# A graph layer's destination rows: made per pair in the loop from copied columns of x, in place of a table and its loads

## What is computed

```python
def _cgconv(x, src, dst, edge_attr, Wf, bf, Ws, bs, gamma, beta, rmean, rvar):
    z = jnp.concatenate([x[dst], x[src], edge_attr], axis=-1)
    msg = jax.nn.sigmoid(z @ Wf + bf) * jax.nn.softplus(z @ Ws + bs)
    n = x.shape[0]
    summed = jax.ops.segment_sum(msg, dst, num_segments=n)
    cnt = jax.ops.segment_sum(jnp.ones((dst.shape[0],), x.dtype), dst, num_segments=n)
    out = summed / jnp.maximum(cnt, 1.0)[:, None]
    out = (out - rmean) * jax.lax.rsqrt(rvar + BN_EPS) * gamma + beta
    return out + x
...
x = _layernorm(x + _L0_gnn_ref(x, edge_index, edge_attr_64, ...), axis=-1)
```

## Time and profile before

| | |
|---|---|
| timed runs (3) | median 2142.03 us, 2137.26 to 2143.15 |
| span of the profiled execution | 2795.4 us |
| its own time beside the span | not given apart from the span |
| granted TensorE clock, mean | 0.747 |
| TensorE (PE) busy | 1618.1 us, 58% |
| VectorE (DVE) busy | 1685.4 us, 60% |
| ScalarE (ACT) busy | 1379.6 us, 49% |
| GpSimd (POOL) busy | 1541.2 us, 55% |
| moved by DMA | 401.73 MB, mean 144 GB/s |

### The profile page before, as it was taken

How to read it: one execution, slowest core, us unless ns; L and a number is a source line. 1 busy time by engine, 2 the same in 40 slices (tenths; PEclk the granted TensorE clock), 3 DMA queues, 4 the chain that set the end, 5 groups by cost and what they waited for, 6 DMA issues and landing times. The chain is left out here.

```text
span 2795.4 us, 33286 instructions
## 1 busy us (share of the span) xinstructions
PE 1618.1 (58%) x7507; PEld 1390.7 (50%) x7507; DVE 1685.4 (60%) x3576; ACT 1379.6 (49%) x2083; POOL 1541.2 (55%) x1590
## 2 busy tenths in 40 slices
PE   6565665566666666666726555555555454454554
PEld 5454555556555565555625444454444444454443
...
GB/s 314 124 148 136 135 147 143 138 151 137 138 143 145 151 145 144 138 155 129 224 152 138 133 138 138 135 144 127 144 138 131 134 138 137 131 144 135 133 136 62
DMA packets 232010, 401.73 MB, mean 144 GB/s; under 512 B 71586, under 2 KB 154906, under 8 KB 231863
## 3 DMA queue, kind: packets, MB, share of 16 engines
...
...
## 5 line engine op out<-in xcount | busy, mean ns | idle before, releaser
L333 POOL DMA_INDIRECT pre<-s_rows,ends x1568 | 1520.5, 970 | 1125.4 <-DVE soft_ps L584 557.2
L378 PE MATMUL pre_ps<-rhs,lhs 128*128 128x256 f32 x3136 | 1102.5, 513 | 1108.1 <-DVE lhs L564 581.1
L378 PEld LDWEIGHTS pre_ps<-rhs,lhs 128*128 128x128 f32 x3136 | 766.6, 256 | 1275.7 <-issue 685.3
L438 ACT ACTIVATE pre<-pre 128x512 f32<-128x512 f32 x392 | 247.5, 631 | 1323.7 <-DVE pre L580 1064.5
L600 DVE TENSOR_TENSOR sums<-sums,sum_ps 128x128 f32 (+1 forms) x784 | 196.4, 251 | 907.8 <-remote 765.2
L388 PEld LDWEIGHTS sum_ps<-hot,msg 128*128 128x128 f32 x3136 | 526.5, 230 | 49.9 <-DVE msg L591 7.3
L388 PE MATMUL sum_ps<-hot,msg 128*128 128x64 f32 x3136 | 489.2, 304 | 7.0 <-DVE msg L591 6.8
L580 DVE TENSOR_TENSOR pre<-pre_ps,pre 128x1024 f32<-128x1024 f32 x392 | 477.6, 1218 | 23.9 <-PE pre_ps L378 22.6
L443 ACT ACTIVATE logs<-pre 128x1024 f32<-128x1024 f32 x392 | 414.7, 1058 | 12.3
L564 DVE TENSOR_SCALAR lhs<-lhs,base_f,part 64x256 f32<-64x256 int32 x784 | 322.2, 454 | 48.1 <-issue 35.6
L591 DVE TENSOR_TENSOR msg<-soft_ps,logs 128x512 f32<-128x512 f32 x392 | 271.1, 692 | 13.3
...
## 6 DMA issues: line engine op xcount, KB each, us to landing
lhs<-dge_and_destination_cols SPq DMA_DIRECT2D x196, 512.0 KB
rhs<-d_rows SPq DMA_DIRECT2D x784, 64.0 KB
pre<-s_rows,ends POOLq DMA_INDIRECT x1568
s_rows<-pre SPq DMA_DIRECT2D x24, 512.0 KB, 5.6
d_rows<-logs SPq DMA_DIRECT2D x12, 512.0 KB
d_rows<-msg SPq DMA_DIRECT2D x8, 512.0 KB
...
d_rows<-hot SPq DMA_DIRECT2D x4, 512.0 KB
```

The source lines that it names most:

```text
L333: nc.gpsimd.indirect_dma_start(pre[:, slot(k, j), i, 0:F2], None, s_dram, bass.IndirectOffsetOnAxis(ap=ends[:, k, j * TILES + i, 0:1], axis=0)
L378: ins = nc.tensor.matmul(pre_ps[:, j % 2, i, :], lhs[:, j // 2, edges], rhs[:, j, i // 2, :], start=True, stop=True)
L438: nc.scalar.activation(pre[:, at, :, F2:3 * F], pre[:, at, :, F:F2], ACT.Abs).then_inc(s_abs[j], 1)
```

## The change

- `d_rows`, its 25 double tiles a layer, their bias adds, their stores and SP's loads of 64 rows a pair go.
- VectorE copies, four steps ahead, the 64 columns of x of each pair's window into `x_cols` (`window_cols`, at an address from a register), between and behind its two adds into `sums`. The registers of the next group's bases are read at the start of a group, beside those of the group before. The adds of both pairs now come ahead of L580.
- TensorE makes, two steps ahead (`dst_rows`), one product of the 128 copied columns (both pairs) with the destination weights, and one bf16 product that adds the bias out of three bf16 parts (`bias_b`), into `dst_ps`.
- ScalarE copies the two halves of `dst_ps`, 64x256 each, into `rhs` (`rows`). A copy keeps its partitions, so the first pair has its one-hot and destination rows on partitions 0 to 63 and the second on 64 to 127; the edge features and weights take the other half, and `edge_cols` is laid out so.
- `sum_ps` has one half only, and a window's sum waits for the adds of one step back in place of two. The counts of layer 1 are two matmuls of 2x64 columns in place of four of 64.
- SP stores all of `s_rows` before it reads the plan; the first edges are loaded behind the fourth store. GpSimd reads the plan before it waits for the stores.

The diff, cut to its core:

```diff
+LEAD = 2
...
+        x_cols = sb("x_cols", [P, SLOTS, PAIRS, WIN], F32)
         hot = sb("hot", [P, SLOTS, TILES, WIN], F32)
         msg = sb("msg", [P, SLOTS, TILES, F], F32)
         pre_ps = ps("pre_ps", [P, 2, TILES, F2], F32)
-        sum_ps = ps("sum_ps", [P, 2, PAIRS, 2, P], F32)
+        sum_ps = ps("sum_ps", [P, PAIRS, 2, P], F32)
         soft_ps = ps("soft_ps", [P, 2, TILES, F], F32)
+        dst_ps = ps("dst_ps", [P, F2], F32)
...
+        hot_rows = [slice(0, WIN), slice(FE, P)]
+        fea_rows = [slice(WIN, P), slice(0, FE)]
...
+        def ahead(g, j):
+            over = (j + LEAD) // SLOTS
+            return (g + over if over else g), (j + LEAD) % SLOTS
...
-            def load_rows(j, bases):
-                for q in range(PAIRS):
-                    sp.dma_start(rhs[FE:P, j, q, :], d_dram[bass.ds(bases[PAIRS * j + q], WIN), :]
-                                 ).then_inc(d_in[j], 16)
-
-
             for k in range(EARLY):
                 load_ends(k, k)
-            for c in range(8):
-                sp.wait_ge(s_copied, 2 * c + 2)
+            for c in range(STORES):
+                sp.wait_ge(s_copied, min(2 * c + 2, DOUBLES))
                 store_rows(sp, s_dram, s_stage, c, s_out)
+                if c == 3:
+                    for j in range(0, SLOTS, 2):
+                        load_edges(j, j * STEP)
             if first:
                 sp.wait_ge(table_out, 48)
             bodies = n_bodies(sp)
             at = sp.value_load(t["choice"][:, 1:2], min_val=0, max_val=GENERAL_AT * ROW)
-            load_table(at)
             for k in range(EARLY):
                 load_base(at + k * ROW, k)
-            for c in range(8, STORES):
-                sp.wait_ge(s_copied, min(2 * c + 2, DOUBLES))
-                store_rows(sp, s_dram, s_stage, c, s_out)
-            for j in range(0, SLOTS, 2):
-                load_edges(j, j * STEP)
-            for c in range(STORES):
-                sp.wait_ge(d_added, min(2 * c + 2, DOUBLES))
-                store_rows(sp, d_dram, d_stage, c, d_out)
-            for r in range(len(d_stage)):
-                sp.wait_ge(d_out[r], 16 * len(range(r, STORES, len(d_stage))))
+            load_table(at)
...
-                bases = entries(1, GPAIRS, NPAD - WIN)
...
-                    load_rows(j, bases)
-                    load_rows(j + 1, bases)
...
+            bodies = n_bodies(pool)
             for r in range(len(s_stage)):
                 pool.wait_ge(s_out[r], 16 * len(range(r, STORES, len(s_stage))))
-            bodies = n_bodies(pool)
...
+            def dst_rows(g, j):
+                done(pe, s_cols, g, j, 0)
+                done(pe, s_rows, g, j, 1)
+                nc.tensor.matmul(dst_ps[:], x_cols[:, j].rearrange("p q w -> p (q w)"), t["w_node"][:, layer - 1, 0:F2],
+                                 start=True, stop=False)
+                nc.tensor.matmul(dst_ps[:], t["ones_b"][:], t["bias_b"][:, layer - 1, :], start=False, stop=True
+                                 ).then_inc(s_dst[j], 1)
 
             def product(b, k, j):
                 g = group_no(b, k)
                 done(pe, s_hot_t, g, j, 0)
                 done(pe, edge_in, g, j // 2, 0, 16)
-                done(pe, d_in, g, j, 0, 16 * PAIRS)
+                done(pe, s_rows, g, j, 0)
...
-                done(pe, s_added, g, j, 2)
+                done(pe, s_added, g, j, 1)
                 for q in range(PAIRS):
                     for i in range(2):
-                        ins = nc.tensor.matmul(sum_ps[:, j % 2, q, 0, 0:WIN], msg[:, j, 2 * q + i, :],
+                        ins = nc.tensor.matmul(sum_ps[:, q, 0, 0:WIN], msg[:, j, 2 * q + i, :],
                                                hot[:, j, 2 * q + i, :], start=i == 0, stop=i == 1)
-                    if first:
-                        for i in range(2):
-
-                            ins = nc.tensor.matmul(sum_ps[:, j % 2, q, 1, 0:WIN], t["ones_b"][:],
-                                                   hot[:, j, 2 * q + i, :].bitcast(BF16)[:, 1::2],
-                                                   start=i == 0, stop=i == 1)
+                if first:
+                    halves = hot[:, j].bitcast(BF16).rearrange("p (q i) (w c) -> p q i w c", i=2, c=2)
+                    for i in range(2):
+                        ins = nc.tensor.matmul(sum_ps[:, :, 1, 0:WIN], t["ones_b"][:],
+                                               halves[:, :, i, :, 1], start=i == 0, stop=i == 1)
                 ins.then_inc(s_sum[j], 1)
...
+                    dst_rows(*ahead(group_no(b, k), j))
+            for j in range(LEAD):
+                dst_rows(0, j)
...
+            def rows(g, j):
+                done(act, s_dst, g, j, 0)
+                done(act, s_prod, g, j, SLOTS)
+                for q in range(PAIRS):
+                    ins = nc.scalar.copy(rhs[hot_rows[q], j, q, :], dst_ps[hot_rows[q], :])
+                ins.then_inc(s_rows[j], 1)
...
+                    rows(*ahead(g, j))
                     absolute(g, j, slot(k, j))
                     exponents(g, j, slot(k, j))
                     logarithms(g, j)
                     gate(g, j)
+            for j in range(LEAD):
+                rows(0, j)
...
+                then(nc.vector.memset(t["bias_b"][:], 0.0))
+                then(nc.vector.tensor_copy(parts[0], t["bias"][:]))
+                then(nc.vector.tensor_tensor(rest, t["bias"][:], parts[0], ALU.subtract))
+                then(nc.vector.tensor_copy(parts[1], rest))
+                then(nc.vector.tensor_tensor(rest, rest, parts[1], ALU.subtract))
+                then(nc.vector.tensor_copy(parts[2], rest))
+                for i, part in enumerate(parts):
+                    then(nc.vector.tensor_copy(t["bias_b"][32 * i:32 * i + 1], part[32 * i:32 * i + 1]))
+                v.sem_inc(bias_split, 1)
...
-                v.wait_ge(tables_done, DOUBLES + i + 1)
-                if c >= len(d_stage) and i % 2 == 0:
-                    v.wait_ge(d_out[c % len(d_stage)], 16 * (c // len(d_stage)))
-                nc.vector.tensor_tensor(d_stage[c % len(d_stage)][:, i % 2 * 2:i % 2 * 2 + 2, :],
-                                        table_ps[:, (DOUBLES + i) % 4],
-                                        t["bias"][:, layer - 1, :].unsqueeze(1).to_broadcast([P, 2, F2]), ALU.add
-                                        ).then_inc(d_added, 1)
...
-                    ins = nc.vector.tensor_scalar(lhs[WIN:P, j // 2, at], lhs[WIN:P, j // 2, at].bitcast(I32),
-                                                  base_f[WIN:P, k, PAIRS * j + q:PAIRS * j + q + 1],
-                                                  t["part"][WIN:P, 0:1], ALU.subtract, ALU.is_equal)
+                    ins = nc.vector.tensor_scalar(lhs[hot_rows[q], j // 2, at],
+                                                  lhs[hot_rows[q], j // 2, at].bitcast(I32),
+                                                  base_f[hot_rows[q], k, PAIRS * j + q:PAIRS * j + q + 1],
+                                                  t["part"][hot_rows[q], q:q + 1], ALU.subtract, ALU.is_equal)
...
-                ins = nc.vector.tensor_tensor(into, into, sum_ps[:, j % 2, q, 0:rows, 0:WIN], ALU.add)
+                ins = nc.vector.tensor_tensor(into, into, sum_ps[:, q, 0:rows, 0:WIN], ALU.add)
...
+            def window_cols(g, j, q, at):
+                if q == 0:
+                    done(v, s_dst, g, j, 0)
+                ins = nc.vector.tensor_copy(x_cols[:, j, q, :], x[:, bass.ds(at[PAIRS * j + q], WIN)])
+                if q == PAIRS - 1:
+                    ins.then_inc(s_cols[j], 1)
...
+                if live(0):
+                    window_cols(g, j, 0, cols_at)
+                if four_back:
+                    add_up(four_back[0], four_back[2], 1, sum_at)
+                if live(0):
+                    window_cols(g, j, 1, cols_at)
...
-                if four_back:
-                    add_up(four_back[0], four_back[2], 1, sum_at)
...
+            def base_loaded(k, turn):
+                if isinstance(turn, int):
+                    v.wait_ge(base_in[k], turn * 16 + 16)
+                else:
+                    v.wait_ge(base_in[k], turn * 16)
+                v.sem_inc(passed, 1)
...
+                if k < BODY - 1:
+                    base_loaded(k + 1, b if isinstance(b, int) else b + 1)
+                else:
+                    base_loaded(0, 1 if isinstance(b, int) else b + 2)
+                cols_at = load_bases((k + 1) % BODY)
...
+            base_loaded(0, 0)
+            cols_at = load_bases(0)
+            for j in range(SLOTS):
+                for q in range(PAIRS):
+                    ins = nc.vector.tensor_copy(x_cols[:, j, q, :], x[:, bass.ds(cols_at[PAIRS * j + q], WIN)])
+                ins.then_inc(s_cols[j], 1)
...
+    edge_cols = np.empty((P, EPAD // STEP, PAIRS, PAIR), features.dtype)
```

(2 more changed lines are left out.)

103 lines of the change are left out of this document (55 added, 48 removed).

## The result

The changed kernel takes 2136.47 us (median of 9 runs, 2131.03 to 2138.22), the kernel before beside it 2142.60 us (9 runs, 2137.26 to 2145.20): ratio 0.997, interval 0.9961 to 0.9979. That is 6.1 us or 0.3% faster. The forecast was 2122 us: its direction was right, the gain was less than a third of what it gave. Ratios and intervals leave out executions more than 1.5% above the fastest of their kernel, six of the twelve of `e1` among them; medians are of all.

A forecast was written before the change was run, and what follows sets the result against it. The prediction held that GpSimd's gathers, issued one after another at 5.01 us a step, bound the kernel. 2142 us less 10 for ring waits and 10 for earlier starts, all else 0, gave 2122 us, range 2085 to 2180.

The forecast's parts named there:

- the 765.2 us: VectorE's idle time ahead of the add into `sums` in the earlier profile; most of it held absent from timed runs.
- The gap of 25.1 us: What the median has above GpSimd's unstalled chain of 2116.9 us; to be filled by slow gathers and ring waits.
- slow gathers: Gathers taking 0.970 us in the mean instead of 0.95: 15 us taken of 31 possible.
- the ring: GpSimd's waits early in each layer, its seven slots full while the destination table is still being stored: 10 us taken.
- Term 1: Row loads, `d_rows` and its stores go; traffic was hidden, GpSimd's ring waits end: -10 us, between 0 and -39.
- Term 2: Start of each layer: source table stored sooner, first gather earlier: -5 us a layer, -10 together, between -14 and +3.
- Term 3: VectorE's two copies a step, added distance and register loads: 0, hidden by GpSimd's 5.01 us step; 196 us uncovered.
- Terms 4 to 6: TensorE's new products and ScalarE's copies, sums in one bank, bias parts and lane tables at the start: 0 each.
- this rival: TensorE at its lower clock for half the steps or more: 2138 us at half, 2436 at three quarters; chance 0.05.
- the 57 priced: Upper end for gathers slowed by starting under VectorE's copies: +57 us, 0 taken; as a rival 2179 us, chance 0.10.
- The rival "no difference": Timed ring waits were nil and the edge loads eat the earlier stores' gain: 2136 to 2148 us, chance 0.15.

The follow-up runs named there:

- e1: The kernel before with only the change's new order of stores and loads at the start, where the unaltered one takes 2789 us: 2781.74 us, ratio 0.9913.
- e16: The kernel before, unaltered, run again and traced on a chip like that of the comparison: 2140.09 us, ratio 0.9998.
- e18: The changed kernel with the old order at the start and the edge loads last: 2139.08 us, 0.9996 of the kernel before.
- e20: The changed kernel with VectorE making every second later copy of the source table's rows in place of ScalarE: 2133.92 us, 0.9977 of the kernel before.
- e10: The changed kernel with the first edge loads behind the last source store, where the kernel before takes 2789 us: 2841.30 us, ratio 1.0173.
- e15: The changed kernel with the bias product made twice in each step on TensorE: 2131.72 us, 0.9965 of the kernel before.

## Why the prediction was right in its direction and wrong in its size

- **What bounds the kernel: right.** GpSimd's chain of gathers does, on the chips of the comparison: 1568 gathers at 946 ns in the median with 0.30 us of issue, and only 10.2 us of other waits in the kernel before. The forecast had left out the 765.2 us as not being in a timed run. That is right for the timed runs shown, but not as it was meant, as something of the profiled execution: on the 2790 chips every traced execution has 653 to 765 us of them.
- **The gap of 25.1 us: filled with too much.** I put 15 us on slow gathers and 10 on the ring. In the trace of `e16` the layers take 990.47 + 989.69 us from first gather to last, 18.0 above 1566 x 1.253: 9.4 are slow gathers (1499.0 - 1568 x 0.95), 6.0 the ring's waits less their issue, and the rest is issue just over 0.30 us. Another 2.8 us lie behind the last gathers of the layers. (The waits taken whole would have passed the median by 45 us, not 46.) The 15.97 and 23.06 us of the earlier trace rows are 2.02 and 4.57 here.
- **Term 1, ring waits -10 us: the step that failed most.** The waits ended as said (10.2 to 0.3 us), but both layers together got only 2.6 us shorter, and in `e18` 0.3. A gather that had waited now has 0.30 us of issue like all others: 14 x 0.30 = 4.2 us were in those 10.2 anyway (issue, without the two starts, went from 472.6 to 476.8 us). And the gathers got slower, 1499.0 to 1502.4 us, 3.4 more. I had taken a wait whole and the disturbance at 0.
- **Term 2, an earlier start, -5 us in each layer: the mechanism right, the size too large in layer 2.** It gave 4.7 us in layer 1 and 2.5 in layer 2, less 1.1 us at the layers' ends, whose cause isn't shown. The pause at the choice did cost what it should, through the backlog of stores and not through a later last issue; that one is set by TensorE's 0.86 us for two tiles (`e20`). The other 1.4 and 1.2 us are the register that GpSimd reads ahead of its wait. The first gather came at 37.6 us, not 36: the last copy of the table ended at 30.8 instead of 29.5 us, and the store took 5.5 us behind the edge loads. `e10`, with the last copy at 29.8 us and no edge loads ahead, has it at 35.7. For layer 2 the forecast had no row, only layer 1's 5 us again.
- **Term 3, copies hidden: right, and its price was too high.** 222 ns each, within 70 to 280; uncovered 94.5 us for the copies and 123 in all, not 196. One wait of GpSimd for `soft_ps`, of 0.3 us, was left.
- **Terms 4 to 6 at 0: right** on a 2140 chip (for TensorE's part, `e15`). TensorE's two new products take 0.9 us a step ((263.7 + 109.0) / 396) and not 0.5, and are hidden all the same. The clock didn't fall: 0.832 before, 0.903 after, with TensorE's busy share at 73% instead of 70%. That is what the prediction had against this rival: TensorE has fewer idle stretches.
- **The gathers beside the copies.** They take 956 ns before and 958 after, and with each copy made twice 972 against 969 on a 2790 chip. 3.4 us of the 57 priced came, and hardly from the copies: in the trace of the changed kernel 102 gathers start under a copy, 948 ns in the mean, 970 at most. 2.5 of the 3.4 us lie on the gathers that start under `hot_transposed` (259 of 981 ns; before, 252 of 972). The Trainium skill, "SBUF — State Buffer", section "SBUF: two separate sides", would have fp32 copies lock GpSimd out; gathers that overlap a copy take 946.5 ns and those that don't 946.1 (without those that start under the one-hot rows), so the measurement decides against a sizeable price here.
- **The rival "no difference"** had the right range, and half of its reasons: the ring's waits were nearly worthless, but the edge loads took only part of what the earlier stores gave.

The six moments add up: 4.7 + 2.6 + 2.5 - 1.1 = 8.7 us of this pair, where the forecast had 20. Of the 11.3 us that are missing, term 1 has 7.4, term 2 has 2.8 and the layers' ends 1.1.
